# Loading the second stage's first tiles into the first stage's input and output buffers

## The chip, the cores and the metric

The kernel runs on one core of a Trainium2 chip. The time is the device time of one execution in microseconds (us); a timing is the median over its runs. The profile is that of one more execution, whose own time is given beside its span.

## The reference

The input x is 32 images of 256 channels and 56 x 56 pixels (M = 3136), float32. Two layers are computed. Cut to what matters:

```python
# layer 0, over all images at once: im is (256, 32*3136)
im = relu(x); mn = mean(im); im = im - mn
p = clip(u.T @ im, -clampVal, clampVal)
scale = 255 / (max(p) - min(p))            # one per row, over all images
p = round((p - min(p)) * scale) / scale + min(p)
p = u @ p;  y = p - mean(p) + mn
# layer 1, per image
h = relu(bn(w_conv1 @ y)); d = relu(bn(w_dr @ h + b_dr))
cov = covariance of d over the pixels;  att = sigmoid(w_fc @ rowconv(bn(cov)) + b_fc)
out = y * att
```

The minimum and the maximum of p over all 32 images have to be known before anything can be quantised, and so the work falls into stages.

## The kernel before

The two sets of 128 channels (K = 2) lie on the 128 partitions. The kernel has three blocks, and each ends with a barrier that all five engines meet.

**First stage** (a span of 565 us): p = u.T @ relu(x) for all images. An image goes through in four pieces (SUBS = 4) of 784 pixels (S). SP, the engine that only issues transfers here, loads each piece into `xs[:, k]` once GpSimd has read the piece that was there (`split_done`). ScalarE applies the relu in place and makes the coarse part `xh`, GpSimd makes the rest `xl`, TensorE multiplies, and VectorE moves the result out of PSUM while it takes maximum and minimum. For the first NL = 28 images the result goes into one of four buffers `po[k]` and from there SP stores it to DRAM (`p0_dram`); `p_stored[k]` counts the stores that have landed. Two of these buffers are `po_low`, two lie in the long-lived buffer `late`. The last RES = 4 images stay in SBUF (`p_res`) and are not stored. They are taken one after every seven stored images, so that the last image of the stage is one that stays: behind the last store there is a whole image of work with no transfer in it.

**Second stage** (566 to 803 us): every p is quantised to a byte so that the bytes can be summed, and the weights of the third stage are prepared. First VectorE reduces the statistics, and TensorE multiplies the mean by u (`shift_ps`); from these come `lo` and `qa`, the offset and the scale of the quantisation, which every tile needs. Then the 56 stored tiles (28 images x 2 channel sets, each 128 x 3136 numbers, 1568 KB) are brought back through four places (TILES = 4) `pt[:, t]`: SP issues four loads at the stage's start (L393), and then one more whenever VectorE has quantised the tile in that place (`quantised`, L398). VectorE quantises a tile into `qt` (L530), and ScalarE reads the bytes and sums them (L470). The four kept images are quantised and summed in the same way without a load (L537, L464).

The order on each engine is written out by hand. Between the groups of four tiles (`two_samples`) stand the steps of the weight preparation, and they pass back and forth between the engines: ScalarE copies `w1u_ps` (L481) behind the first four sums; VectorE scales the weights with it (L549, L550); ScalarE takes absolute values (L485, L486) behind the next five sums; TensorE sums them (L435); VectorE makes scales of them (L556 to L577); ScalarE takes `absv` (L490) behind five more sums; TensorE L446, VectorE L592 to L600, TensorE L450, VectorE L603 to L611. Only then does VectorE enter the loops in which nothing but tiles is worked on.

**Third stage** (803 us to the end): for each image the outputs and the attention are computed from the bytes, which are made anew from a reload of p. TensorE bounds it.

Of the kernel before, what the change touches and what calls it, by code (L numbers as in the profile page):

```python
# [29 lines left out]
P = 128  # L30
# [9 lines left out]
def wait_from(eng, semaphore, value):  # L40

    if not (isinstance(value, int) and value <= 0):
        eng.wait_ge(semaphore, value)


def layer_kernel(nc, x, u, clamp, w1, g1, b1, wdr, b_dr, g_dr, be_dr, g_row, be_row,
                 w_row, b_row, w_fc, b_fc, out):
    N, C, HH, WW = x.shape
    M = HH * WW
    K = C // P  # L50
    J = w_row.shape[1]
    RES = 4
    NL = N - RES
# [4 lines left out]
    p0_dram = nc.dram_tensor("p0_scratch", [N, K, P, M], F32, kind="Internal").ap()  # L58
    p0_v = p0_dram.rearrange("n k p m -> n p k m")

    with ExitStack() as ctx:
        def sb(name, shape, dt=F32, stack=ctx):
            return stack.enter_context(nc.sbuf_tensor(name, shape, dt))
# [4 lines left out]
        def sem(name):  # L68
            return ctx.enter_context(nc.semaphore(name))
# [51 lines left out]
        lo = sb("lo", [P, K])  # L121
# [8 lines left out]
        SUBS = 4  # L130
        S = M // SUBS
# [12 lines left out]
        stats = ExitStack()  # L144
        xsum = sb("xsum", [P, K, N * SUBS], stack=stats)
        pmax = sb("pmax", [P, K, N * SUBS], stack=stats)
        pmin = sb("pmin", [P, K, N * SUBS], stack=stats)

        x_loaded = [sem(f"x_loaded{k}") for k in range(SUBS)]
        p_stored = [sem(f"p_stored{k}") for k in range(SUBS)]  # L150
        u_split, relu_done, high_done, split_done = (sem("u_split"), sem("relu_done"), sem("high_done"),
                                                     sem("split_done"))
# [1 line left out]
        scaled = sem("scaled")  # L154

        with ExitStack() as a:
            xs = sb("xs", [P, SUBS, K, S], stack=a)
            xh = sb("xh", [P, 2, K, S], F32R, stack=a)
            xl = sb("xl", [P, 2, K, S], F32R, stack=a)
            po_low = sb("po_low", [P, 2, K, S], stack=a)  # L160
            po_late = late[:, 0:2 * K * S].rearrange("p (b k s) -> p b k s", b=2, k=K)
            po = [po_low[:, 0], po_low[:, 1], po_late[:, 0], po_late[:, 1]]
            uh = sb("uh", [P, K, C], F32R, stack=a)
# [8 lines left out]
            @block.sync  # L172
            def _(sp):
                sp.dma_start(u_sb[:], u.rearrange("(k p) j -> p k j", p=P)).then_inc(u_loaded, 16)
                for k in range(SUBS):
                    sp.dma_start(xs[:, k], x_v[0, :, :, k * S:(k + 1) * S]).then_inc(x_loaded[k], 16)
                for dst, src in [
                    (w1_sb[:], w1.rearrange("(k p) o -> p k o", p=P)), (wdr_sb[:], wdr),
                    (wrow_sb[:], w_row), (wfc_sb[:], w_fc.rearrange("(k p) n -> p k n", p=P)),
                    (brow_sb[:], b_row.rearrange("(p j) -> p j", j=J)),  # L180
                ]:
                    sp.dma_start(dst, src).then_inc(params_loaded, 16)
                for dst, src in [(cv, clamp), (g1_sb, g1), (b1_sb, b1), (bfc_sb, b_fc)]:
                    for k in range(K):
                        sp.dma_start(dst[:, k:k + 1], src[k * P:(k + 1) * P].rearrange("(p o) -> p o", o=1)
                                     ).then_inc(params_loaded, 16)
                for dst, src in [(bdr_sb, b_dr), (gdr_sb, g_dr), (bedr_sb, be_dr), (grow_sb, g_row),
                                 (berow_sb, be_row)]:
                    sp.dma_start(dst[:], src.rearrange("(p o) -> p o", o=1)).then_inc(params_loaded, 16)

                def load(n, turn, k):

                    sp.wait_ge(split_done, SUBS * (turn - 1) + k + 1)
                    sp.dma_start(xs[:, k], x_v[n, :, :, k * S:(k + 1) * S]).then_inc(x_loaded[k], 16)

                def store(n, k):
                    sp.wait_ge(p_ready, SUBS * n + k + 1)
                    sp.dma_start(p0_v[n, :, :, k * S:(k + 1) * S], po[k]).then_inc(p_stored[k], 16)


                def load_and_store(n_load, n_store, turn, first=False):
                    for k in range(SUBS):
                        load(n_load, turn, k)
                        if k > 0:
                            store(n_store, k - 1)
                        elif not first:
                            store(n_store - 1, SUBS - 1)

                def group(r, more):
                    load_and_store(PER * r + 1, PER * r, (PER + 1) * r + 1, first=True)  # L210
                    with sp.Fori(1, PER - 1) as s:
                        load_and_store(PER * r + s + 1, PER * r + s, (PER + 1) * r + s + 1)
                    load_and_store(NL + r, PER * r + PER - 1, (PER + 1) * r + PER)
                    if more:
                        load(PER * r + PER, (PER + 1) * r + PER + 1, 0)
                    store(PER * r + PER - 1, SUBS - 1)
                    if more:
                        for k in range(1, SUBS):
                            load(PER * r + PER, (PER + 1) * r + PER + 1, k)

                with sp.Fori(0, RES - 1) as r:
                    group(r, True)
                group(RES - 1, False)

            @block.scalar
            def _(act):
# [123 lines left out]
                    resident_sample(r, (PER + 1) * r + PER)  # L350


        TILES = 2 * K
        PAIRS = NL // 2

        p_loaded = [sem(f"p_loaded{t}") for t in range(TILES)]
        mean_done, shift_done = sem("mean_done"), sem("shift_done")
        res_quantised, res_summed = sem("res_quantised"), sem("res_summed")
        quantised, summed = sem("quantised"), sem("summed")
# [3 lines left out]
        rows_made, rows_spread = sem("rows_made"), sem("rows_spread")  # L363

        with ExitStack() as b:
            pt = sb("pt", [P, TILES, M], stack=b)
            qt = sb("qt", [P, TILES, M], U8, stack=b)
            hi = sb("hi", [P, K], stack=b)
            same = sb("same", [P, K], stack=b)
# [17 lines left out]

            @block.sync
            def _(sp):
                for k in range(SUBS):  # L390
                    sp.wait_ge(p_stored[k], 16 * NL + 16)
                for t in range(TILES):
                    sp.dma_start(pt[:, t], p0_dram[t // K, t % K]).then_inc(p_loaded[t], 16)  # L393

                with sp.Fori(0, NL - 2, 2) as n:
                    for t in range(TILES):
                        sp.wait_ge(quantised, K * n + t + 1)
                        sp.dma_start(pt[:, t], p0_dram[n + 2 + t // K, t % K]).then_inc(p_loaded[t], 16)  # L398

            @block.tensor  # L400
            def _(pe):
# [52 lines left out]
            def _(act):  # L454
# [12 lines left out]
                def two_samples(p):  # L467
                    for t in range(TILES):
                        act.wait_ge(quantised, TILES * p + t + 1)
                        nc.scalar.activation(qt[:, t], qt[:, t], ACT.Copy,  # L470
                                             accum_out=qsum[:, t % K, bass.ds(2 * p + t // K, 1)]
                                             ).then_inc(summed, 1)

                def round_of_pairs(i):
                    for h in range(2):
                        resident_tile(i, h)
                        two_samples(2 * i + h + 1)
# [13 lines left out]
                with act.Fori(1, RES) as i:  # L491
                    round_of_pairs(i)
                with act.Fori(2 * RES + 1, PAIRS) as p:
                    two_samples(p)

            @block.vector
            def _(dve):
# [28 lines left out]
                def two_samples(i):  # L526
                    for t in range(TILES):
                        dve.wait_ge(p_loaded[t], 16 * (i + 1))
                        wait_from(dve, summed, TILES * (i - 1) + t + 1)
                        nc.vector.tensor_scalar(qt[:, t], pt[:, t], lo[:, t % K:t % K + 1],  # L530
                                                qa[:, t % K:t % K + 1], ALU.subtract, ALU.mult).then_inc(quantised, 1)

                def resident_tile(i, h):
# [6 lines left out]
                def round_of_pairs(i):  # L540
                    for h in range(2):
                        resident_tile(i, h)
                        two_samples(2 * i + h + 1)

                two_samples(0)

                dve.wait_ge(turned_read, 2)
# [3 lines left out]
                last.then_inc(scaled_w, 1)  # L551
                resident_tile(0, 0)
                two_samples(1)

                dve.wait_ge(sums_done, 1)
# [59 lines left out]
                with dve.Fori(1, RES) as i:  # L615
                    round_of_pairs(i)
                with dve.Fori(2 * RES + 1, PAIRS) as p:
                    two_samples(p)
# [26 lines left out]
        with ExitStack() as c_:  # L645
# [285 lines left out]
            def _(dve):  # L931
                steps = [0]

                def settle(ins):
                    steps[0] += 1
                    ins.then_inc(prepare_step, 1)
                    dve.wait_ge(prepare_step, steps[0])
# [18 lines left out]
                nc.vector.memset(gg[:], 1.0)  # L956
                dve.wait_ge(summed, TILES * PAIRS)
                settle(nc.vector.tensor_reduce(mq, qsum[:], AX_X, ALU.add))
# [117 lines left out]
```

## Time and profile before

| | |
|---|---|
| median of 3 runs | 1931.46 us (1931.35 to 1931.91) |
| the profiled execution's own time | 1932.07 us |
| its span, first to last instruction | 1930.3 us |
| TensorE busy | 1677.6 us (87%) |
| VectorE busy | 1530.7 us (79%) |
| ScalarE busy | 1498.2 us (78%) |
| GpSimd busy | 460.4 us (24%), all in the first stage: 459.6 us of it in its 128 pieces |
| mean granted TensorE clock | 0.935 of full speed |
| first, second, third stage | to 565.6, 565.6 to 802.8, from 802.8 us |

In the profile PE is TensorE, PEld its weight loads, DVE is VectorE, ACT is ScalarE, POOL is GpSimd, SP issues the transfers; a q behind an engine's name is its sequencer. Times are counted from the span's start. A line L530 is line 530 of the kernel before. What an idle engine waited for is written with an arrow, as [1.44 <-DMA ...].

### The profile page before, as it was taken

What the parts mean: (1) busy time and instruction counts of PE and PEld (TensorE: products, weight loads), DVE (VectorE), ACT (ScalarE), POOL (GpSimd) and SP (SyncE); (2) the same over time, 40 slices, a digit from 0 to 9 for tenths busy, and PEclk for the clock granted to TensorE, in tenths of its full rate; (3) what the DMA queues carried; (4) which work ended last, traced back from release to release, by engine and by line L of the source; (5) the groups of instructions that cost most, each with busy time, mean ns of one, the idle gap of its engine ahead of it and who ended that gap; (6) DMA issues with size and microseconds to landing.
All of it is one profiled execution on the core that took longest, in us unless ns stands there. A gap on an engine that the chain in (4) does not pass through costs nothing.

```text
span 1930.3 us, 40083 instructions
## 1 busy us (share of the span) xinstructions
PE 1677.6 (87%) x13394; PEld 1319.8 (68%) x13394; DVE 1530.7 (79%) x2801; ACT 1498.2 (78%) x2270; POOL 460.4 (24%) x135
## 2 busy tenths in 40 slices
PE   8999999999981000289999999999999999999998
PEld 8999999999981000156666666666676666666664
DVE  5888888888875664466888888888888888888883
ACT  6777777777756897568788887878878888787886
POOL 6888888888840000000000000000000000000000
PEclk9999999999985555599999999999999999999999
DMA  9998999989968899601364554645546455554634
GB/s 326 377 365 315 372 339 343 374 316 366 374 260 346 351 425 426 280 2 68 128 230 164 194 195 154 236 154 210 181 164 224 160 213 175 177 207 160 228 113 201
DMA packets 139341, 477.35 MB, mean 247 GB/s; under 512 B 10528, under 2 KB 33184, under 8 KB 124192
## 3 DMA queue, kind: packets, MB, share of 16 engines
q1 hardware_dynamic: 139296, 476.75, 67.2%
q8 instruction: 28, 0.46, 0.1%
q14 instruction: 17, 0.14, 0.0%
HBM read 284.04 MB, written 192.68 MB: 247 GB/s over the span
## 4 chain that ended last, share of the span: by engine, by line
PE 55%; ACT 1%; DVE 1%; issue 1%; ACTq 0%
PE y_ps L829 18%; PE z_ps L855 17%; PE d_ps L805 13%; PE cov_ps L786 5%; PE ch_ps L840 1%; ACT h L896 1%; ACT hh L901 0%; PE ch_ps L818 0%; PE ch_ps L817 0%; DVE g L1046 0%; PE cov_ps L789 0%; ACT p_res L924 0%; DVE hl L1037 0%; PE ch_ps L764 0%; PE cov_ps L770 0%
## 5 line engine op out<-in xcount | busy, mean ns | idle before, releaser
L278 POOL TENSOR_TENSOR xl<-xs,xh 128x1568 fp32r<-128x1568 f32 x128 | 459.6, 3591 | 97.8 <-ACT xh L238 97.8
L1037 DVE TENSOR_TENSOR hl<-h,hh 128x1024 f16<-128x1024 f32 (+2 forms) x224 | 244.1, 1090 | 102.9 <-ACT hh L901 102.7
L829 PE MATMUL y_ps<-qr,udh 128*128 128x512 f16 (+2 forms) x896 | 313.5, 353 | 4.0 <-ACT p_res L924 3.6
L855 PE MATMUL z_ps<-qr,wl 128*128 128x512 f16 (+2 forms) x896 | 314.1, 354 | 0.0
L855 PE MATMUL z_ps<-qr,wh 128*128 128x512 f16 (+2 forms) x896 | 314.0, 353 | 0.0
L829 PE MATMUL y_ps<-qr,udl 128*128 128x512 f16 (+2 forms) x896 | 313.0, 352 | 0.0
L924 ACT ACTIVATE p_res<-y_ps,att_cy 128x512 f32<-128x512 f32 (+2 forms) x448 | 298.2, 713 | 9.5 <-PE y_ps L829 4.5
L238 ACT ACTIVATE xh<-xs 128x1568 fp32r<-128x1568 f32 x128 | 194.1, 1517 | 140.6 <-PE pp L295 140.6
L896 ACT ACTIVATE h<-z_ps,sb_h 128x512 f32<-128x512 f32 (+2 forms) x448 | 264.4, 627 | 30.6 <-PE z_ps L855 26.8
L805 PE MATMUL d_ps<-vh,hh 128*128 128x128 f16 (+1 forms) x1600 | 282.3, 220 | 2.5 <-DVE hl L1037 2.3
L805 PE MATMUL d_ps<-vh,hl 128*128 128x128 f16 (+1 forms) x1600 | 281.6, 219 | 0.0
L805 PE MATMUL d_ps<-vl,hh 128*128 128x128 f16 (+1 forms) x1600 | 281.5, 219 | 0.0
L295 PE MATMUL pp<-xh,uh 128*128 128x392 f32 x1024 | 267.6, 342 | 9.2 <-ACT xh L238 9.2
L295 PE MATMUL pp<-xh,ul 128*128 128x392 f32 x1024 | 266.9, 342 | 0.0
L888 ACT ACTIVATE gg<-g 128x512 f16<-128x512 f32 (+1 forms) x224 | 130.8, 584 | 175.2 <-DVE g L1046 175.2
L329 DVE TENSOR_REDUCE pmin<-pp 128x784 f32 x256 | 248.3, 970 | 0.0
L901 ACT ACTIVATE hh<-h 128x1024 f16<-128x1024 f32 (+2 forms) x224 | 212.8, 950 | 7.1
L232 ACT ACTIVATE xs<-xs 128x784 f32<-128x784 f32 x256 | 215.3, 843 | 3.7 <-DMA xs<-in_x_dram 3.7
L295 PE MATMUL pp<-xl,uh 128*128 128x392 f32 x1024 | 204.8, 342 | 0.0
L295 PEld LDWEIGHTS pp<-xh,uh 128*128 128x128 f32 x1024 | 188.8, 189 | 9.2 <-issue 9.2
L295 PEld LDWEIGHTS pp<-xh,ul 128*128 128x128 f32 x1024 | 189.2, 189 | 0.0
L295 PEld LDWEIGHTS pp<-xl,uh 128*128 128x128 f32 x1024 | 185.5, 188 | 0.0
(164 smaller groups left out, 2820.7 us busy)
## 6 DMA issues: line engine op xcount, KB each, us to landing
xs<-in_x_dram SPq DMA_DIRECT2D x128, 784.0 KB, 6.8
out_dram<-p_res SPq DMA_DIRECT2D x31, 3136.0 KB, 10.3
pt<-p_scratch SPq DMA_DIRECT2D x56, 1568.0 KB, 12.9
p_res<-p_scratch SPq DMA_DIRECT2D x112, 512.0 KB, 4.6
p_scratch<-po_low SPq DMA_DIRECT2D x56, 784.0 KB, 7.7
p_scratch<-late SPq DMA_DIRECT2D x56, 784.0 KB, 7.7
p_res<-p_scratch SPq DMA_DIRECT2D x56, 384.0 KB, 3.2
p_res<-p_scratch SPq DMA_DIRECT2D x28, 320.0 KB, 3.3
```

The costliest lines, as they stand in the source:

```text
L232: last = nc.scalar.activation(xs[:, k, m], xs[:, k, m], ACT.Relu, accum_out=xsum[:, m, bass.ds(g, 1)])
L238: nc.scalar.activation(xh[:, k % 2], xs[:, k], ACT.Copy).then_inc(high_done, 1)
L278: nc.gpsimd.tensor_tensor(xl[:, k % 2], xs[:, k], xh[:, k % 2].bitcast(F32), ALU.subtract).then_inc(split_done, 1)
L295: last = nc.tensor.matmul(pp[:, k % 2, m, c, 0:SC], lhs, rhs[:, c * SC:(c + 1) * SC], start=first and n == 0, stop=final and n == len(part ...
L329: nc.vector.tensor_reduce(pmin[:, m, bass.ds(g, 1)], p_psum(k, m), AX_XY, ALU.min).then_inc(psum_read, 1)
L805: last = nc.tensor.matmul(d_ps[0:q, par, t], lhs, rhs, start=n == 0, stop=n == len(parts) - 1)
L829: last = nc.tensor.matmul(y_ps[:, m, 0:widths[c]], part[:, k, m * P:(m + 1) * P], qr[:, slot, k, columns(c)], start=k == 0 and part is udh ...
L855: last = nc.tensor.matmul(z_ps[:, m, 0:w], part[:, k, m * P:(m + 1) * P], qr[:, a, k, columns(s)], start=k == 0 and part is wh, stop=k == ...
L896: nc.scalar.activation(h32[:, par, m, 0:w], z_ps[:, m, 0:w], ACT.Relu, bias=sb_h[:, m:m + 1]).then_inc(z_read, 1)
L901: nc.scalar.activation(hh[:, par, :, 0:w], h32[:, par, :, 0:w], ACT.Copy).then_inc(hh_done, 1)
L924: nc.scalar.activation(yo[:, slot, m, columns(c)], y_ps[:, m, 0:widths[c]], ACT.Identity, scale=att_cy[:, m, 0:1], bias=att_cy[:, m, 1:2]) ...
L1037: nc.vector.tensor_tensor(hl[:, par, :, 0:w], h32[:, par, :, 0:w], hh[:, par, :, 0:w], ALU.subtract).then_inc(h_split, 1)
```

## The change

The tile places of the second stage are laid over buffers of the first. A new buffer `early`, 128 x 3 x 3136, lives through both. In the first stage `early[:, 0]` is the pair `po_low`, and `early[:, 1:3]` are the four x pieces: pieces 0 and 1 fill the second of the three parts, pieces 2 and 3 the third. In the second stage the three parts are the places of tiles 0, 1 and 2; the fourth is the new `late_tile`, which only the second stage has. The total is what it was, since `xs`, `po_low` and `pt` are no longer buffers of their own.

The first three loads move from the start of the second block to the end of the first block's SP program. Tile 0 waits for all stores of the first stage to have landed, tile 1 for GpSimd to have read pieces 0 and 1 of the last image, tile 2 for it to have read all four. The fourth load stays where it was.

```diff
+        EARLY = TILES - 1
+        early = sb("early", [P, EARLY, M], stack=stats)
...
-            xs = sb("xs", [P, SUBS, K, S], stack=a)
+            xs = early[:, 1:3].rearrange("p t m -> p (t m)").rearrange("p (u k s) -> p u k s", u=SUBS, k=K)
...
-            po_low = sb("po_low", [P, 2, K, S], stack=a)
+            po_low = early[:, 0].rearrange("p (b k s) -> p b k s", b=2, k=K)
...
+                def load_p(t):
+                    sp.dma_start(early[:, t], p0_dram[t // K, t % K]).then_inc(p_loaded[t], 16)
+
+                for k in range(SUBS):
+                    sp.wait_ge(p_stored[k], 16 * NL + 16)
+                load_p(0)
+                sp.wait_ge(split_done, SUBS * (N - 1) + 2)
+                load_p(1)
+                sp.wait_ge(split_done, SUBS * N)
+                load_p(2)
...
-            pt = sb("pt", [P, TILES, M], stack=b)
+            late_tile = sb("late_tile", [P, M], stack=b)
+            pt = [early[:, t] for t in range(EARLY)] + [late_tile[:]]
...
-                for k in range(SUBS):
-                    sp.wait_ge(p_stored[k], 16 * NL + 16)
-                for t in range(TILES):
-                    sp.dma_start(pt[:, t], p0_dram[t // K, t % K]).then_inc(p_loaded[t], 16)
+                sp.dma_start(pt[EARLY], p0_dram[EARLY // K, EARLY % K]).then_inc(p_loaded[EARLY], 16)
```

Here is SP's program around the barrier between the first and the second stage, before the change. L194 loads an x piece, L198 stores a p piece, L156 is the branch out of the first block, and L393 and L398 are the loads of tiles.

```order
L194 DMA xs<-in_x_dram 128x2x784 [waits split_done]
L198 DMA p_scratch<-late 128x2x784 [waits p_ready] x2
L156 UNCONDITIONAL_BRANCH
L388 UNCONDITIONAL_BRANCH [waits barrier_Pool_Activation_PE_DVE_SP_release]
L393 DMA pt<-p_scratch 128x3136 [waits p_stored2,p_stored3,p_stored1,p_stored0]
L393 DMA pt<-p_scratch 128x3136 x3
L395 UNCONDITIONAL_BRANCH
L395 ISA
L398 ISA [waits quantised]
L398 DMA pt<-p_scratch 128x3136
```

And the same place after it, where L201, L205, L163 and L411 are the former L194, L198, L156 and L398, and L234 and L406 the former L393.

```order
L201 DMA early<-in_x_dram 128x2x784 [waits split_done]
L205 DMA p_scratch<-late 128x2x784 [waits p_ready] x2
L234 DMA early<-p_scratch 128x3136 [waits p_stored2,p_stored3,p_stored1,p_stored0]
L234 DMA early<-p_scratch 128x3136 [waits split_done] x2
L163 UNCONDITIONAL_BRANCH
L404 UNCONDITIONAL_BRANCH [waits barrier_Pool_Activation_PE_DVE_SP_release]
L406 DMA late_tile<-p_scratch 128x3136
L408 UNCONDITIONAL_BRANCH
L408 ISA
L411 ISA [waits quantised]
L411 DMA early<-p_scratch 128x3136
```

Three loads with their waits now stand ahead of the barrier; one stays behind it, and the loop of reloads is as before.

VectorE's program at the start of the second stage, after the last step that makes `lo` and `qa`, before the change:

```order
L524 TENSOR_SCALAR qa<-hi 128x2
L530 TENSOR_SCALAR qt<-pt,lo,qa 128x3136 [waits p_loaded0,vec_step]
L530 TENSOR_SCALAR qt<-pt,lo,qa 128x3136 [waits p_loaded1]
L530 TENSOR_SCALAR qt<-pt,lo,qa 128x3136 [waits p_loaded2]
L530 TENSOR_SCALAR qt<-pt,lo,qa 128x3136 [waits p_loaded3]
L549 TENSOR_SCALAR late<-late,inv 128x256 [waits turned_read]
```

And after it:

```order
L537 TENSOR_SCALAR qa<-hi 128x2
L543 TENSOR_SCALAR qt<-early,lo,qa 128x3136 [waits p_loaded0,vec_step]
L543 TENSOR_SCALAR qt<-early,lo,qa 128x3136 [waits p_loaded1]
L543 TENSOR_SCALAR qt<-early,lo,qa 128x3136 [waits p_loaded2]
L543 TENSOR_SCALAR qt<-late_tile,lo,qa 128x3136 [waits p_loaded3]
L562 TENSOR_SCALAR late<-late,inv 128x256 [waits turned_read]
```

The order and the waits are the same; only the places of the tiles have other names. The programs of ScalarE, TensorE and GpSimd differ in names alone as well.

## Rows read from the trace of the kernel before

**Rows 1.** Busy time by stretch; behind the engines granted TensorE clock, DMA share, GB/s:

```profile
551.50:565.60 14.10, 10.67 (x60) 10.36 (x59) 11.83 (x21) 6.83 (x25) 6.73 (x2) 0.97 0.00 2
...
615.00:620.00 5.00, 2.08 (x2) 0.50 (x2) 4.96 (x11) 1.87 (x1) 0.00 (x0) 0.50 0.01 2
...
640.00:645.00 5.00, 0.00 (x0) 0.00 (x0) 5.00 (x3) 3.04 (x3) 0.00 (x0) 0.50 0.17 30
...
650.80:797.60 146.80, 0.00 (x0) 0.00 (x0) 81.90 (x45) 129.51 (x91) 0.00 (x0) 0.50 1.00 422
```

**Rows 2.** VectorE in order of time (start, duration, what, idle before and its releaser):

```profile
571.57 0.16 DVE L524 TENSOR_SCALAR qa<-hi 128x2 f32<-128x2 f32 x1
573.16 1.91 DVE L530 TENSOR_SCALAR qt<-pt,lo,qa 128x3136 uint8<-128x3136 f32 x1 [1.44 <-DMA pt<-p_scratch]
...
584.42 1.91 DVE L530 TENSOR_SCALAR qt<-pt,lo,qa 128x3136 uint8<-128x3136 f32 x1 [1.87 <-DMA pt<-p_scratch]
589.80 0.35 DVE L549 TENSOR_SCALAR late<-late,inv 128x256 f32<-128x256 f32 x1 [3.46 <-ACT late L481]
```

**Rows 3.** ScalarE in order of time over the same stretch:

```profile
571.32 1.02 ACT L460 ACTIVATE late<-wfc_ps 128x1024 f32<-128x1024 f32 x1 [1.95 <-PE wfc_ps L421]
575.11 2.82 ACT L470 ACTIVATE qt<-qt 128x3136 uint8<-128x3136 uint8 x1 [2.76 <-DVE qt L530]
...
586.37 2.82 ACT L470 ACTIVATE qt<-qt 128x3136 uint8<-128x3136 uint8 x1 [0.87 <-DVE qt L530]
...
589.19 0.58 ACT L481 ACTIVATE late<-w1u_ps 128x512 f32<-128x512 f32 x1
...
595.61 2.80 ACT L470 ACTIVATE qt<-qt 128x3136 uint8<-128x3136 uint8 x1
...
606.81 0.61 ACT L485 ACTIVATE u_sb<-late 128x512 f32<-128x512 f32 x1
```

**Rows 4.** The later steps of the weight preparation, from the same view of three engines:

```profile
571.08 3.62 PE L427 MATMUL w1u_ps<-late,u_sb 128*128 128x256 f32 x8
...
607.99 1.01 PE L435 MATMUL shift_ps<-ones,w_sb 128*128 128x1 f32 x4 [33.29 <-ACT w_sb L486]
...
613.30 0.16 DVE L556 TENSOR_TENSOR small<-b_sb,shift_ps 128x2 f32<-128x2 f32 x1 [11.87 <-PE shift_ps L435]
...
618.13 2.82 ACT L464 ACTIVATE q_first<-q_first 128x3136 uint8<-128x3136 uint8 x1 [10.19 <-DVE q_first L537]
...
633.64 0.16 DVE L592 SCALAR_TENSOR_TENSOR small<-shift_ps,small 128x1 f32<-128x1 f32 x1 [4.81 <-PE shift_ps L446]
...
641.72 7.37 DVE L530 TENSOR_SCALAR qt<-pt,lo,qa 128x3136 uint8<-128x3136 f32 x4
```

**Rows 5.** VectorE where the tiles alone are left, and its last tile:

```profile
654.18 1.91 DVE L530 TENSOR_SCALAR qt<-pt,lo,qa 128x3136 uint8<-128x3136 f32 x1 [1.45 <-DMA pt<-p_scratch]
...
797.58 1.91 DVE L530 TENSOR_SCALAR qt<-pt,lo,qa 128x3136 uint8<-128x3136 f32 x1 [1.85 <-DMA pt<-p_scratch]
```

**Rows 6.** SP's issues, its wait at the barrier, GpSimd's last piece:

```profile
542.91 4.69 SPq L198 DMA_DIRECT2D p_scratch<-late  x2
565.69 2.24 SPq L393 DMA_DIRECT2D pt<-p_scratch  x4
...
SPq L156 <- PEq L156: 17.7, 1, 17.7
...
555.37 3.58 POOL L278 TENSOR_TENSOR xl<-xs,xh 128x1568 fp32r<-128x1568 f32 x1 [0.72 <-ACT xh L238]
```

**Rows 7.** Issue to landing (the tile loads; 540 to 575 us), instruction transfers (570 to 576 us):

```profile
DMA to landing us min/median/max: 6.3/12.9/17.4
...
pt<-p_scratch SPq DMA_DIRECT2D x4, 1568.0 KB, 12.4
p_scratch<-late SPq DMA_DIRECT2D x2, 784.0 KB, 6.5
...
q8 instruction: 1, 0.02, 0.9%
```

More of the change, by code:

```diff
@@ L147, in layer_kernel @@
         pmin = sb("pmin", [P, K, N * SUBS], stack=stats)
+        TILES = 2 * K
+        PAIRS = NL // 2
+        EARLY = TILES - 1
+        early = sb("early", [P, EARLY, M], stack=stats)
+        assert SUBS == TILES and SUBS * S == M
         x_loaded = [sem(f"x_loaded{k}") for k in range(SUBS)]
+        p_loaded = [sem(f"p_loaded{t}") for t in range(TILES)]
         p_stored = [sem(f"p_stored{k}") for k in range(SUBS)]
@@ L350, in _ @@
                     resident_sample(r, (PER + 1) * r + PER)
-        TILES = 2 * K
-        PAIRS = NL // 2
-        p_loaded = [sem(f"p_loaded{t}") for t in range(TILES)]
         mean_done, shift_done = sem("mean_done"), sem("shift_done")
@@ L397, in _ @@
                         sp.wait_ge(quantised, K * n + t + 1)
-                        sp.dma_start(pt[:, t], p0_dram[n + 2 + t // K, t % K]).then_inc(p_loaded[t], 16)
+                        sp.dma_start(pt[t], p0_dram[n + 2 + t // K, t % K]).then_inc(p_loaded[t], 16)
             @block.tensor
@@ L529, in two_samples @@
                         wait_from(dve, summed, TILES * (i - 1) + t + 1)
-                        nc.vector.tensor_scalar(qt[:, t], pt[:, t], lo[:, t % K:t % K + 1],
+                        nc.vector.tensor_scalar(qt[:, t], pt[t], lo[:, t % K:t % K + 1],
                                                 qa[:, t % K:t % K + 1], ALU.subtract, ALU.mult).then_inc(quantised, 1)
```

## Prediction

> **What bounds the kernel now.** I read the table of the engines first: TensorE is busy for 87% of the span, but the change touches none of its work. The stretches come next, since a busy share is a mean over stages. In the second stage TensorE is nearly idle, and its time is set in one part by the transfers and in another by the weight preparation. From 650.80 to 797.60 us the DMA share is 1.00 at 422 GB/s; from 615 to 620 it is 0.01 and from 640 to 645 it is 0.17 [rows 1]. The reader is to see in this that the stage has two regimes. Up to 641.7 us the transfers run ahead of the engines, fill the four places and stop. After that they are the limit: VectorE's tile at 654.18 and the last at 797.58 wait for a load, with 38 steps between them, so (797.58 - 654.18) / 38 = 3.77 us a tile [rows 5].
>
> Second, the order of time on VectorE and ScalarE at the stage's start. VectorE makes `qa` at 571.57 and then waits 1.44 us for the first load; it starts the fourth tile at 584.42, after 1.87 us of waiting for its load; that is 11.26 us for three steps, the 3.77 of the loads again. Then it waits 3.46 us for ScalarE's copy L481, until 589.80 [rows 2]. ScalarE sums the first tile at 575.11 and the fourth at 586.37, idle before that one for 0.87 us, and makes the copy at 589.19 [rows 3]. This chain was late because of loads. Behind it there is not one load on the path up to 641.72: ScalarE's sums follow each other without a gap from 595.61 to the absolute values at 606.81 [rows 3]; TensorE (607.99), VectorE (613.30), ScalarE (618.13), VectorE (633.64) wait for one another, and VectorE's four tiles from 641.72 take 7.37 us with no wait inside them [rows 4].
>
> Third, SP: it issued the last two stores from 542.91 on and stood at the barrier for 17.7 us [rows 6], while the DMA share was 0.00 for 14.1 us [rows 1].
>
> **The change part by part.** All times below are in the profiled execution.
>
> Issue of the early loads. The last store was issued at about 542.91 + 4.69 - 0.39 = 547.2, and the last two took 6.5 us in the median to land [rows 6, 7]: 553.7. Then tile 0 is issued; tile 1 with it, since GpSimd read piece 1 of the last image two pieces before the one it starts at 555.37; tile 2 at 555.37 + 3.58 = 558.95 [rows 6]. SP needs under a microsecond for each issue (2.24 us for four [rows 6]) and is at the barrier by about 560, 5 us before it opens. Nothing is queued behind these waits on SP, since its last store is out, and no other transfer is wanted until 565.6.
>
> Landing. Over the 56 tile loads the time to landing was 6.3 us at least and 17.4 at most, queueing behind others included; the four at the stage's start had a median of 12.4 [rows 7]. The first of those four was issued at 565.69 and used at 573.16 [rows 2, 6], 7.5 us. So tile 0 lands near 561, tile 1 near 565, tile 2 near 569 (3.77 after the one before it or 7.5 after its issue, whichever is later, with some for queueing), and `late_tile`, alone in the queue from 565.7, near 573.2.
>
> VectorE. L521 to L524 come with steps of 0.2 us behind one another where one waits for the one before, so tile 0 starts at 571.57 + 0.20 = 571.77 in place of 573.16. Four tiles back to back take 7.37 us [rows 4], a step of (7.37 - 1.91) / 3 = 1.82: they start at 571.8, 573.6, 575.4 and 577.2. Every load above is there by then, the tightest by 4 us.
>
> ScalarE is now the slower of the two. It is free at 571.32 + 1.02 = 572.34 and starts 0.04 us behind a tile's end (573.16 + 1.91 against 575.11): at 573.72. Its own step is (606.81 - 595.61) / 4 = 2.80 [rows 3], so the fourth sum starts at 582.12 and copy L481 at 584.94. What the copy reads was made by TensorE by 571.08 + 3.62 = 574.70 [rows 4]. VectorE goes on 0.61 us after the copy's start, at 585.55 in place of 589.80. The saving: 1.39 us from the earlier first tile, 2.86 us because four sums start within 8.40 us in place of 11.26; **4.25 us**. The whole 15 us that the first four loads took is not to be had: 11.3 of it, three tiles by 3.77, is taken off SP's queue, and ScalarE's sums, hidden beside the loads before, become the limit after 4.25 of it.
>
> From there to 641.72. Each link moves by the same 4.25 us if no load is late. The loads of the second four follow the quantising of the first four, from 573.7 on: with 7.5 us for the first and 3.77 for each further one they land at 581.2, 585.0, 588.7 and 592.5, and VectorE wants them at 588.4, 590.3, 592.1 and 593.9 (592.67, 594.49 and so on before, each less 4.25; 592.67 is 589.80 with its four scalings and one kept tile). ScalarE, which is the path here, wants the last of them quantised only by 599.8. For the third and the fourth group both the places and their users move together, and the queue ran dry before both already [rows 1]. TensorE's few products at 607.99 come after 33.29 us of idleness [rows 4]; now it is 29, and the granted clock there is 0.50 in every one of these stretches [rows 1], so they cost the same.
>
> From 641.72 on. The four places are full in both kernels when VectorE gets there, so the head start of the loads is used up: a fifth tile can't be loaded ahead. The 40 tiles left go at 3.77 each from a start that is 4.25 us earlier. The last tile, the barrier and the third stage move with it.
>
> The other edits (a view in place of a buffer, other addresses, the same four places) change no instruction in number or shape; I cost them at 0. The traffic of the early loads lies beside the last image's work. GpSimd's step there is 3.58 us at a DMA share of 0.00 [rows 6, 1], and 459.6 / 128 = 3.59 in the mean over all its pieces, nearly all with the queues full, so I take nothing for it.
>
> Bounds. Above: if `lo` and `qa` were not the limit either, ScalarE's sums could start at 572.34, 1.4 us earlier, but they need them; so 4.3 is the upper end of this mechanism. Below: a late `late_tile` costs nothing until it is quantised after 582.12, so until it lands after 580.2, which is 14.5 us behind its issue; at the longest landing time of the trace, 17.4, it would cost 2.9 us, and the gain would be 1.4. I take the row of a load issued into an empty queue, 7.5 us, as the nearest. To both sides I add 0.6 us, the spread of the three runs.
>
> The sum: 1932.07 - 4.25 = 1927.8 us for an execution like the profiled one. That one is 0.61 us over the median of the runs, so the median is forecast at 1931.46 - 4.25 = 1927.2 us, 0.22% faster. A change of 0.2%, 3.9 us, is about what a measurement of this kernel can tell from none.
>
> **The rivals.** *The transfers set the whole stage.* The share of 1.00 over 147 us speaks for it. Then all three tiles count: 3 x 3.77 = 11.3 us, 1920.2 us. Against it are the two dry stretches of the queue [rows 1] and the 10.19 us and 11.87 us that ScalarE and VectorE wait for one another in between [rows 4]. Chance 0.04.
>
> *A smaller gain.* Some link between 589.80 and 641.72 doesn't follow, or a load lands late: 1.4 to 3.5 us are left, 1928 to 1930. No row shows a link that hangs on something else, but the view names only the last releaser of each wait. Chance 0.12.
>
> *The barrier waits for the loads.* If the end of a block holds until the transfers of SP's queue have landed, the second stage starts when tile 2 is in. Landed at 569 that is 3.4 us later than 565.6, and the gain is 0.9 us, 1930.6; at 12.4 us behind its issue at 559 it is 571.4, a loss of 1.5, 1933.0; the gain is gone from a landing at 569.9 on. The rows say little against it, as the stores before had landed 12 us before the barrier. In its favour I see only that no row excludes it. Chance 0.05.
>
> *Slower: code waits behind the loads.* All engines branch into the second block at 565.6, until now with empty queues. If one of them must fetch code there, and the fetch stands in line behind two tile loads, the stage's first steps, which lead to `qa`, come 2 x 3.77 = 7.5 us later; less 4.25 that is a loss of 3.3 us, 1934.8. It decides from a delay of 4.25 us on. Against it: an instruction transfer lies in the stretch from 570 to 576, with the queues full [rows 7], and no engine stood still for it there. The Trainium skill ("DMA: Bandwidth & Descriptors", section "Queues, rings and completion order") says that each DMA engine takes turns between the queue rows that have work, a packet at a time; by that rule the fetch would not stand behind whole tiles, and the time would be that of the forecast. The trace agrees as far as it goes, by that one transfer. Chance 0.04.
>
> **How the numbers follow.** The forecast, 1927.2 us, has 0.75 with its own range 1926.6 to 1928.2. The range for 8 in 10 reaches up into the smaller gain and leaves out the rest: 1926.2 to 1929.6. Faster by over 0.2% means under 1927.6: some 0.87 of the forecast's chance, since it lies only 0.4 us beyond, and the case of 11 us: 0.69. Within 0.2%: the rest of the forecast, the smaller gain and nearly all of the barrier's and the code's cases: 0.27. Slower by over 0.2% needs a delay of over 8 us: 0.04.
>
> **What would show it.** In the profile of the changed kernel: VectorE's first tile near 571.8 with no wait for a load, the next three 1.8 us apart; ScalarE's four sums without a gap; L562 (the former L549) near 585.6; the group of four at 641.72 now near 637.5; the last tile near 793.3; the barrier still at 565.6. I am wrong if the barrier opens later, if VectorE still waits for a load among the first four, if the DMA share does not fall to nothing once more around 611 to 616, or if the 4.25 us at 585.6 are not the same 4.25 us at 637.5.

## The result and the profile after

The changed kernel takes 1926.10 us in the median of 8 runs (1924.81 to 1927.39); the kernel before, run beside it, 1931.40 us (1929.61 to 1932.67, 8 runs). The ratio is 0.9972, 95% interval 0.9961 to 0.9983: 5.4 us faster, between 3.3 and 7.5. Forecast were 1927.2 us and a gain of 4.25 us; the gain lies in the interval, the time 0.1 us under the lower end of my range, 1926.2. With eight runs the median is the middle of the fourth and the fifth, 1925.34 and 1926.86, and no run took a time between these two. The profiled execution took 1926.86 us, its span is 1925.1 us.

The stretches of the changed kernel, in the columns of [rows 1] (the last three are granted clock, DMA share and GB/s):

```profile
551.50:565.60 14.10, 10.66 (x60) 10.36 (x59) 11.81 (x20) 6.69 (x24) 6.58 (x2) 0.95 0.84 338
...
610.00:615.00 5.00, 2.07 (x2) 0.50 (x2) 4.90 (x13) 1.28 (x1) 0.00 (x0) 0.50 0.00 2
635.00:640.00 5.00, 0.00 (x0) 0.00 (x0) 5.00 (x6) 2.43 (x1) 0.00 (x0) 0.50 0.00 0
...
646.50:793.30 146.80, 0.00 (x0) 0.00 (x0) 82.14 (x45) 129.66 (x91) 0.00 (x0) 0.50 1.00 421
```

Against [rows 1] the reader sees the DMA engines busy ahead of the barrier, which they were not, and the same two dry stretches, some 5 us earlier. VectorE, to be set beside [rows 2]:

```profile
571.42 0.16 DVE L537 TENSOR_SCALAR qa<-hi 128x2 f32<-128x2 f32 x1
571.62 5.56 DVE L543 TENSOR_SCALAR qt<-early,lo,qa 128x3136 uint8<-128x3136 f32 x3
577.09 1.91 DVE L543 TENSOR_SCALAR qt<-late_tile,lo,qa 128x3136 uint8<-128x3136 f32 x1
585.38 0.35 DVE L562 TENSOR_SCALAR late<-late,inv 128x256 f32<-128x256 f32 x1 [6.38 <-ACT late L494]
```

The waits for the four loads are gone, and the wait for ScalarE's copy has grown from 3.46 to 6.38 us: the gain of VectorE was 7.3 us at the fourth tile and is 4.4 us behind the copy. ScalarE, beside [rows 3]:

```profile
573.56 2.82 ACT L483 ACTIVATE qt<-qt 128x3136 uint8<-128x3136 uint8 x1 [1.37 <-DVE qt L543]
...
581.98 2.80 ACT L483 ACTIVATE qt<-qt 128x3136 uint8<-128x3136 uint8 x1
...
584.77 0.57 ACT L494 ACTIVATE late<-w1u_ps 128x512 f32<-128x512 f32 x1
```

Its first and fourth sum start 8.42 us apart, against 11.26 before. The later links, beside [rows 4, 5]:

```profile
603.58 1.02 PE L448 MATMUL shift_ps<-ones,w_sb 128*128 128x1 f32 x4 [29.03 <-ACT w_sb L499]
...
608.89 0.16 DVE L569 TENSOR_TENSOR small<-b_sb,shift_ps 128x2 f32<-128x2 f32 x1 [13.26 <-PE shift_ps L448]
...
629.24 0.16 DVE L605 SCALAR_TENSOR_TENSOR small<-shift_ps,small 128x1 f32<-128x1 f32 x1 [4.81 <-PE shift_ps L459]
...
637.33 5.55 DVE L543 TENSOR_SCALAR qt<-early,lo,qa 128x3136 uint8<-128x3136 f32 x3
...
792.99 1.91 DVE L543 TENSOR_SCALAR qt<-late_tile,lo,qa 128x3136 uint8<-128x3136 f32 x1 [1.84 <-DMA late_tile<-p_scratch]
```

The first stage ends at a slightly different time in each execution, so I count from the barrier, that is from VectorE's first reduction behind it:

```profile
565.62 0.42 DVE L506 TENSOR_REDUCE mn<-xsum 128x2 f32<-128x256 f32 x1 [0.33 <-PEq L156]
```

```profile
565.47 0.42 DVE L519 TENSOR_REDUCE mn<-xsum 128x2 f32<-128x256 f32 x1 [0.33 <-PEq L163]
```

The first is before, the second after. The table has these distances for every kernel of the study (us; "weights" is the first scaling behind ScalarE's copy, "last tile" VectorE's last in the second stage).

| kernel | VectorE's first reduction at | first tile | weights | last tile | median us |
|---|---|---|---|---|---|
| before | 565.62 | +7.54 | +24.18 | +231.96 | 1931.40 |
| after | 565.47 | +6.15 | +19.91 | +227.52 | 1926.10 |
| e1, after again | 565.35 | +6.14 | +19.91 | +227.81 | 1925.73 |
| e2, overlay alone | 564.25 | +7.44 | +24.05 | +231.72 | 1931.38 |
| e3, one tile early | 564.91 | +4.49 | +20.21 | +227.95 | 1927.29 (one run) |
| e4, copy earlier | 565.97 | +6.15 | +14.32 | +224.66 | 1924.50 |
| w1, after and matmuls | 565.15 | +4.35 | +18.12 | +225.81 | 1924.50 |
| w2, before and matmuls | 564.58 | +7.28 | +23.89 | +231.52 | 1930.13 |
| a1, after, steps ahead | 564.90 | +4.43 | +12.60 | +208.36 | 1908.66 |
| a2, before, steps ahead | 566.80 | +7.32 | +20.41 | +217.88 | 1917.02 |
| b1, after, both | 564.66 | +4.35 | +12.52 | +208.65 | 1907.65 |

In the two profiled executions the spans differ by 5.2 us. Of that 4.3 us are there at the weights and 4.4 at the last tile. The rest is not shown to be the change's: the barrier is 0.15 us earlier, the third stage gives 0.3 us back (ScalarE's last output starts at 1924.96 before and at 1920.66 after, 4.30 apart), and the last store took 3.9 us to land before and 3.0 after, 0.9 us:

```profile
out_dram<-p_res SPq DMA_DIRECT2D x1, 320.0 KB, 3.9
```

```profile
out_dram<-p_res SPq DMA_DIRECT2D x1, 320.0 KB, 3.0
```

### The profile page after: what moved, and what is told of

Same layout as the page of the kernel before. It is cut to its first block, busy times and chain, and to the rows that moved or that the text cites. A ratio compares the mean times of both kernels' runs of the same rounds, so it can differ in the third digit from the quotient of the medians.

```text
span 1925.1 us, 40083 instructions
## 1 busy us (share of the span) xinstructions
PE 1677.5 (87%) x13394; PEld 1319.3 (69%) x13394; DVE 1530.7 (80%) x2801; ACT 1497.2 (78%) x2270; POOL 459.9 (24%) x135
## 4 chain that ended last, share of the span: by engine, by line
PE 55%; ACT 1%; DVE 1%; issue 1%; ACTq 0%
PE y_ps L842 18%; PE z_ps L868 17%; PE d_ps L818 13%; PE cov_ps L799 5%; ACT h L909 1%; PE ch_ps L853 1%; ACT hh L914 0%; PE ch_ps L831 0%; DVE g L1059 0%; PE ch_ps L830 0%; PE cov_ps L802 0%; ACT p_res L937 0%; DVE hl L1050 0%; ACT gg L901 0%; PE ch_ps L777 0%
## 5 line engine op out<-in xcount | busy, mean ns | idle before, releaser
L297 POOL TENSOR_TENSOR xl<-early,xh 128x1568 fp32r<-128x1568 f32 x128 | 459.1, 3587 | 98.1 <-ACT xh L257 98.1
L257 ACT ACTIVATE xh<-early 128x1568 fp32r<-128x1568 f32 x128 | 194.1, 1516 | 140.2 <-PE pp L314 140.1
L251 ACT ACTIVATE early<-early 128x784 f32<-128x784 f32 x256 | 215.2, 842 | 3.9 <-DMA early<-in_x_dram 3.9
```

The source lines that it names most:

```text
L251: last = nc.scalar.activation(xs[:, k, m], xs[:, k, m], ACT.Relu, accum_out=xsum[:, m, bass.ds(g, 1)])
L257: nc.scalar.activation(xh[:, k % 2], xs[:, k], ACT.Copy).then_inc(high_done, 1)
L297: nc.gpsimd.tensor_tensor(xl[:, k % 2], xs[:, k], xh[:, k % 2].bitcast(F32), ALU.subtract).then_inc(split_done, 1)
```

## The experiments

**e1, the changed kernel again, and e2, the overlay without the early loads** (ratio to before 0.9972, 0.9960 to 0.9983, and 1.0000, 0.9991 to 1.0009). The edit of e2:

```diff
-                load_p(0)
-                sp.wait_ge(split_done, SUBS * (N - 1) + 2)
-                load_p(1)
-                sp.wait_ge(split_done, SUBS * N)
-                load_p(2)
...
-                sp.dma_start(pt[EARLY], p0_dram[EARLY // K, EARLY % K]).then_inc(p_loaded[EARLY], 16)
+                for t in range(TILES):
+                    sp.dma_start(pt[t], p0_dram[t // K, t % K]).then_inc(p_loaded[t], 16)
```

> The changed kernel once more, unaltered. Theory (the early loads bring 4.25 us, fixed by ScalarE's four sums; all beyond it is variation between executions): VectorE goes on behind the copy L494 19.9 us after the barrier, as in the profile of after (585.38 - 565.47), and the loops start 4.25 us earlier than before by the same measure; the five timed pairs differ by 3 to 6 us and the runs of one kernel spread by 2 to 3 us. Rival (a lasting further gain of 1 us from the new layout or from less traffic): the median of the pairs is again 5.2 us or more.

> The change without its early loads: the four tile places lie over the first stage's buffers, but all four loads are issued behind the barrier, as before. Theory: nothing but the early issue matters, so VectorE's first tile starts 7.6 us behind the barrier again, the copy ends the wait 24.2 us behind it, and the time is that of before, within the runs' spread (0 us, -1 to +1). Rival (the layout brings the extra 1 us): 1 us less than before.

The layout brings nothing: e2 is at the time of before, and its first tile waits for its load again. In e1 the profile repeats the 4.27 us at the weights, but the median is 5.3 us under before again, as the rival of e1 had it. Neither interval excludes 4.25 us, so the extra microsecond is not shown by the medians; that it came twice was reason to look closer. The single times say where. The changed kernel's 15 runs (8 and 7) fall into two groups: 8 from 1924.81 to 1925.73, 7 from 1926.86 to 1927.65, and none between. Both profiled executions are of the upper group. Its middle is 1927.4, beside my 1927.2; that of the lower group is 1925.3.

**e3, one tile early.** Only `load_p(0)` stays ahead of the barrier; the other three loads are issued behind it. There is one timed run, so only its profile is used.

> Tile 0 alone is loaded early; tiles 1 to 3 are issued behind the barrier. Theory (ScalarE's sums at 2.80 us a tile take over as the limit): the loads of tiles 1 to 3 land 7.5, 11.3 and 15.0 us behind the barrier, VectorE has them quantised in time for ScalarE's second and third sum, and only the fourth is late, by 0.6 us. VectorE goes on behind the copy 20.5 us after the barrier: 3.6 of the 4.25 us are there with one tile of three. Rival (every early tile brings its equal share): 22.8 us after the barrier, a gain of 1.4 us.

The weights come at +20.21: one tile of three brings 3.97 of the 4.27 us, so equal shares are wrong. It does not show ScalarE's pace, since here the loads still set it. VectorE's third and fourth tile wait for theirs, and ScalarE waits 0.87 us before its fourth sum:

```profile
579.74 1.91 DVE L540 TENSOR_SCALAR qt<-late_tile,lo,qa 128x3136 uint8<-128x3136 f32 x1 [1.87 <-DMA late_tile<-p_scratch]
581.69 2.82 ACT L480 ACTIVATE qt<-qt 128x3136 uint8<-128x3136 uint8 x1 [0.87 <-DVE qt L540]
```

And the first tile starts at +4.49, not at +6.15. That was not expected, and it is the clue:

```profile
564.90 0.30 PE L415 MATMUL w_ps<-ident,w_sb 128*128 128x128 f32 x1 [3.44 <-PEq L163]
...
566.02 1.08 PE L426 MATMUL shift_ps<-mn,u_sb 128*128 128x1 f32 x8
...
567.22 0.16 DVE L522 TENSOR_TENSOR hi<-hi,shift_ps 128x2 f32<-128x2 f32 x1 [1.04 <-PE shift_ps L426]
```

In the profile of after the same three steps read:

```profile
565.46 0.44 PE L418 MATMUL w_ps<-ident,w_sb 128*128 128x128 f32 x1 [3.44 <-PEq L163]
...
567.62 1.70 PE L429 MATMUL shift_ps<-mn,u_sb 128*128 128x1 f32 x8
...
569.44 0.16 DVE L525 TENSOR_TENSOR hi<-hi,shift_ps 128x2 f32<-128x2 f32 x1 [2.70 <-PE shift_ps L429]
```

TensorE had idled for the same 3.44 us in both, but in e3 the clock had not fallen yet when the second stage began. The granted clock from 564 to 566 us and from 566 to 568 us (after first, then e3):

```profile
564.00:566.00 2.00, 0.54 (x3) 0.57 (x4) 1.63 (x5) 0.00 (x0) 0.00 (x0) 0.55 0.88 376
566.00:568.00 2.00, 2.00 (x12) 2.00 (x10) 0.74 (x3) 0.14 (x1) 0.00 (x0) 0.50 0.85 194
```

```profile
564.00:566.00 2.00, 1.10 (x10) 1.13 (x11) 1.63 (x5) 0.00 (x0) 0.00 (x0) 1.00 0.28 50
566.00:568.00 2.00, 2.00 (x15) 2.00 (x14) 0.86 (x6) 1.36 (x3) 0.00 (x0) 0.67 0.82 270
```

The share of 0.50 is 1.2 GHz, that of 1.00 is 2.4 GHz. In e3, where the clock fell between 566 and 568 us, in the middle of these steps, the first tile comes 1.66 us sooner than in after; in w1 below, at 2.4 GHz throughout, 1.80 us. Before, this was hidden: the first tile waited for its load until +7.5. After, these steps are on the path.

**e4, ScalarE's copy earlier.**

```diff
-                two_samples(0)
+                two_samples(0, 0, 2)
                 act.wait_ge(turned, 3)
                 nc.scalar.activation(w1u_t[:], w1u_ps[:], ACT.Copy).then_inc(turned_read, 1)
+                two_samples(0, 2)
```

> The changed kernel, with ScalarE's copy of w1u (L494) moved from behind its four first sums to behind the second. Theory (the four sums ahead of the copy are what is left on the path): VectorE gets its weights at about 14.3 us behind the barrier in place of 19.9, the kept tile no longer makes ScalarE wait 3.03 us, the absolute values come 3.1 us earlier, and the loops start 3.1 us earlier: a time 7 to 8 us under before. Rival (the loads of the second group are the limit as soon as ScalarE is not): the second group waits for its loads and under 1 us comes of it.

Ratio 0.9959 (0.9946 to 0.9972), 7.9 us by the ratio and 6.6 by the medians (1931.06 - 1924.50); 7 to 8 were expected, and the intervals of e4 and after overlap, so the difference between the two kernels rests on the profiles. The weights come at +14.32, where 14.3 was expected, and the last tile 2.9 us earlier than in after. ScalarE's sums ahead of the copy were what limited the gain:

```profile
580.29 0.35 DVE L563 TENSOR_SCALAR late<-late,inv 128x256 f32<-128x256 f32 x1 [0.79 <-ACT late L494]
```

The rival's wait for the second group's loads is there too, 1.30 and 1.87 us on its third and fourth tile, but ScalarE is not held up by it.

**w1 and w2, a busy TensorE up to the barrier**, in the kernel after and in the kernel before. The edit adds work whose result is not used:

```diff
+                pe.wait_ge(psum_read, K * (SUBS * N - 1))
+                for n in range(17):
+                    nc.tensor.matmul(pp[:, 0, 0, 0, 0:SC], uh[:, 0, 0:P], xh[:, 0, 0, 0:SC],
+                                     start=True, stop=True)
```

> The changed kernel with 17 matmuls more at the end of TensorE's first block; they fill the 3.4 us in which it has nothing to do before the barrier, and their result is used by nobody. Theory (the second stage's first steps are now on the path, and they run at whichever clock is granted at the barrier, which is why the runs of after fall into two groups 2 us apart): TensorE's steps up to the product for the shift run at full clock in every execution, VectorE's first tile starts 4.5 us behind the barrier and not 6.15, and the median is that of the lower group of after, 1924.5 to 1925.3. Rival (the two groups come from elsewhere, the third stage for one): two groups again, median 1925.7 to 1926.1.

> The kernel before with the same 17 matmuls. Theory: its first tile waits for its load, which lands 7.5 us behind the barrier whatever the clock, so the quicker first steps bring nothing; first tile 7.4 to 7.6 us behind the barrier, time within 0.5 us of before. Rival (the clock helps either kernel): 1.6 us under before.

w1: ratio 0.9965 (0.9951 to 0.9979), median 1924.50 us, and one group from 1923.97 to 1925.22. The ratio alone does not tell w1 from after, whose interval overlaps; the single group of five and the profile do the telling. The idle time before the barrier's release is 0.42 us and the first steps run at full clock:

```profile
561.54 3.18 PE L336 MATMUL pp<-xh,uh 128*128 128x392 f32 x17
565.14 0.30 PE L423 MATMUL w_ps<-ident,w_sb 128*128 128x128 f32 x1 [0.42 <-PEq L163]
...
566.26 0.95 PE L434 MATMUL shift_ps<-mn,u_sb 128*128 128x1 f32 x8
```

With the first tile 1.80 us sooner than in after the weights come 1.79 us sooner, at +18.12: ScalarE's four sums set that distance. Of the 2.9 us between the two profiled executions 1.7 are there at the last tile; 0.3 lie in the first stage and 0.9 in the third.

w2: ratio 0.9994 (0.9985 to 1.0003). Its steps are as quick, but VectorE waits longer for the load, 2.97 us in place of 1.44:

```profile
566.75 0.16 DVE L517 TENSOR_TENSOR hi<-hi,shift_ps 128x2 f32<-128x2 f32 x1 [0.91 <-PE shift_ps L421]
571.86 1.91 DVE L535 TENSOR_SCALAR qt<-pt,lo,qa 128x3136 uint8<-128x3136 f32 x1 [2.97 <-DMA pt<-p_scratch]
```

The distance to the first tile is 0.12 us under the range expected. The median, 1.3 us under that of before, misses the expected 0.5 and does not settle it by itself: the interval holds 0 and also the rival's 1.6 us. The profile speaks for the theory: w2's last tile is only 0.44 us closer to the barrier than that of before, where w1's is 1.71 closer than that of after.

**a1 and a2, ScalarE's steps ahead of the sums**, again in both kernels. Besides the edit of e4:

```diff
-                resident_tile(0, 0)
-                two_samples(1)
                 act.wait_ge(scaled_w, 1)
                 nc.scalar.activation(absu[:], ud32[:], ACT.Abs)
                 nc.scalar.activation(absw[:], w32[:], ACT.Abs).then_inc(abs_done, 1)
-                resident_tile(0, 1)
-                two_samples(2)
+                resident_tile(0, 0)
+                two_samples(1)
                 act.wait_ge(scaled_v, 1)
                 nc.scalar.activation(absv, v32[:], ACT.Abs).then_inc(abs_done, 1)
+                resident_tile(0, 1)
+                two_samples(2)
```

> The changed kernel with ScalarE's steps of the weight preparation each moved ahead of a group of sums: the copy of w1u behind the second sum, the absolute values of u and w1 ahead of the second group, that of v ahead of the third. Theory (what kept the queue of loads dry around 612 and 638 us were these steps waiting behind the sums): the loads run on with hardly a gap from 573.7 us, the last tile is quantised 209 to 215 us behind the barrier in place of 227.5, the time is 1908 to 1915 us. Rival (with ScalarE's sums at 2.80 us a tile and five tiles a group, ScalarE itself sets the pace): 220 us or more behind the barrier, 1919 us or more.

> The same moves of ScalarE's steps in the kernel before. Theory: now the loads set nearly the whole stage, so the early loads are worth more than the 4.25 us they bring after: the kernel before with the moves has its last tile 216 to 222 us behind the barrier, 7 us later than the changed kernel with them, and takes 1915 to 1922 us. Rival (the early loads bring 4.25 us in any setting): the two differ by 4.25 us. A second one (they bring all three tiles, 11.3 us): they differ by 11.3 us.

a1: ratio 0.9884 (0.9868 to 0.9899), 1908.66 us; a2: 0.9926 (0.9912 to 0.9939), 1917.02 us. The queue of loads is full, or nearly so, where it was dry; in a1:

```profile
605.00:610.00 5.00, 0.00 (x0) 0.00 (x0) 4.86 (x12) 5.00 (x5) 0.00 (x0) 0.50 1.00 418
610.00:615.00 5.00, 1.65 (x2) 0.50 (x2) 3.19 (x15) 2.41 (x2) 0.00 (x0) 0.50 1.01 427
615.00:620.00 5.00, 0.00 (x0) 0.00 (x0) 5.00 (x7) 2.15 (x1) 0.00 (x0) 0.50 0.65 273
```

Early loads are now worth 8.4 us by the medians (1917.02 - 1908.66) and 9.5 at the last tile, neither 4.25 nor 11.3. I had expected 7. The profile of a1 has its first tile at +4.43, which is 1.7 us less than the +6.15 that I had reckoned with, and 7 + 1.7 = 8.7 is in line with it. a1's four times are again two pairs: 1907.21 and 1907.65, the first of them the profiled execution with the full clock, and 1909.66 and 1909.89. The lower pair is 9.6 us under a2's median, the upper 7.2. That the last tile comes 0.6 us earlier than the 209 to 215 probably has the same cause.

**b1, both.**

> Both together on the changed kernel: ScalarE's steps ahead of the groups of sums, and the 17 matmuls before the barrier. Theory: every execution has its first tile 4.35 us behind the barrier, as the profile of w1 had, and the last 208 us behind it; one group of times in place of a1's two (1907.2 and 1907.7, 1909.7 and 1909.9), median 1906.8 to 1907.8. Rival (the matmuls help only while ScalarE's sums are on the path, and the loads are the limit now): median as a1's, 1908.7, and two groups.

1907.65 us, ratio 0.9876 (0.9860 to 0.9893), the fastest kernel here. Its 4 runs lie within 0.6 us (1907.42 to 1908.01), a1's 4 within 2.7. That supports the clock as the cause of the two groups, though four runs each are few, and the medians differ by only 1.0 us.

## Why the prediction's mechanism held, and what failed in it

The early issue: right. SP issued tiles 0 and 1 at 552.9 (I had 553.7) and tile 2 at 558.8, was at the barrier at about 559.4 and waited there 6.0 us:

```profile
552.88 6.28 SPq L234 DMA_DIRECT2D early<-p_scratch  x3
565.42 0.33 SPq L406 DMA_DIRECT2D late_tile<-p_scratch  x1
...
SPq L163 <- PEq L163: 6.0, 1, 6.0
```

The landings: 6.8 and 10.2 us behind the issue for the first two, 8.4 for tile 2 and 7.3 for `late_tile`. So tile 2 landed at 567.2 and `late_tile` at 572.7, ahead of their use at 575.3 and 577.1.

The barrier waiting for the loads: wrong. Tile 2 landed at 558.8 + 8.4 = 567.2, and the barrier opened at 565.47, with 0.33 us between VectorE's last step and its first as before. Code waiting behind the loads: wrong, since `qa` is made 5.95 us behind VectorE's first reduction in both kernels (571.57 - 565.62 and 571.42 - 565.47). The transfers setting the whole stage: wrong in this kernel, the queue ran dry twice; with ScalarE's steps moved (a1 and a2) the early loads bring 9.5 us at the last tile, 1.7 of it by the clock, where this rival had 11.3.

ScalarE's takeover, 4.25 us at the weights, the same at 637.3 and at the last tile: right. By the barrier's clock 4.27, 4.24 (76.10 against 71.86) and 4.44 us were measured. That ScalarE's sums are the reason is shown by e4, in which two sums fewer stand ahead of the copy, and by w1, in which the weights move with the first tile. Expected marks were 571.8, 585.6, 637.5 and 793.3 us, measured 571.6, 585.4, 637.3 and 793.0, with the barrier itself 0.15 us earlier.

What failed is the upper bound of the gain, and with it the lower end of the range: "if `lo` and `qa` were not the limit either, ScalarE's sums could start at 572.34, 1.4 us earlier, but they need them; so 4.3 is the upper end of this mechanism." I took the 6.15 us from the barrier to the first tile from one execution as if they were fixed. They are 6.14 or 6.15 in the three profiles (after, e1, e4) in which the clock had fallen to 1.2 GHz at the barrier. Where it fell later they are 4.43 and 4.49 (a1, e3), and 4.35 where it did not fall in these steps (w1, b1): the gain is up to 1.8 us larger. The copy of `wfc_ps` at 571.32, which I named as ScalarE's earliest start, moves with TensorE's clock too: it is at 5.70 us behind VectorE's first reduction before and at 4.04 in e3. It was in my rows: the stretch from 551.50 has a granted clock of 0.97, the later ones 0.50, so the fall lay near the barrier. What was hidden under a wait for a load could differ from run to run without being seen. The other term that was too small is the 0.6 us for the spread, taken from three runs of before: over 8 runs before alone spread by 3.1 us. None of the four signs by which I had said I would be wrong appeared, and none of them looked at the clock.

So the median is no single number but depends on how many runs fall into which group: 1927.4 us in the group that I forecast, 1925.3 in the other, with 7 and 8 of 15 runs. By how much it missed my range is luck, to either side. With one more of the eight runs in the upper group the median would have been 1926.86 or more, inside the range; with one more in the lower it would have been under 1925.8, as in e1.

How far are the two groups shown to be two moments of the clock's fall? w1's five runs form one group, at or under the lower one; b1's four form one, beside a1's lower pair; and the profiled execution of a1, with the full clock at the barrier, is in that lower pair. The mean granted clock of each run points the same way without separating them: 0.936 or 0.937 in the 8 runs of the lower group, 0.935 in three and 0.936 in four of the upper. But no profiled execution of the unaltered kernel fell into the lower group, so for it the link stays indirect. Nor is the whole distance explained: the first steps give 1.7 to 1.8 us of the 2.1 between the middles of the groups. The kernel before spreads by 3.1 us although its first tile waits for a load, and a2, built on it, has a gap of 1.5 us between its third and fourth time. So part of the spread comes from elsewhere. The traces show two places. One is the first stage, told of in the last section. The other is the third: from VectorE's first step in it to the end of the span it takes 1126.0 us in the profile of w1 and 1127.5 in that of e1.

## What to carry to other kernels

When loads are brought forward, the gain ends where the next engine in line takes over; find its step time and count from when it is free. A stream that is limiting later on gets faster only by as much as its last dry stretch moves, so look first at why it runs dry: here moving three small ScalarE steps ahead of the long sums brought 17 us on top, against 5 us for the loads. And when a wait is removed, whatever was hidden beneath it comes onto the path with all its variation; read its granted clock before calling it constant. Look at the single times too, and not only at their median: a gap among them can mean that two kinds of execution are mixed.

## What the runs showed of the hardware

With the same program on TensorE and the same 3.44 us in which it was idle, the granted clock from 564 to 566 us was 1.00 in one execution (e3) and 0.55 in another (after). The Trainium skill ("TensorE: Matmul & The Clock Gate", section "Part 1: The HAM clock gate") says that what sets the clock does not start anew with the kernel, so that the moment of the change varies between runs. The traces agree, in the fall at the barrier and also in the rise at the start. Two matmuls of the first stage take 0.85 us at 1.2 GHz and 0.52 us at 2.4 GHz. In e2 (the first two lines) the change is between 11.3 and 12.5 us, in before (the other two) between 13.9 and 16.3:

```profile
11.27 0.85 PE L309 MATMUL pp<-xh,ul 128*128 128x392 f32 x2
12.46 0.51 PE L309 MATMUL pp<-xh,ul 128*128 128x392 f32 x2
...
13.94 0.85 PE L295 MATMUL pp<-xh,ul 128*128 128x392 f32 x2
...
16.32 0.52 PE L295 MATMUL pp<-xh,uh 128*128 128x392 f32 x2
```

In e2 the barrier opens 1.4 us earlier than in before (564.25 against 565.62), and the clock falls behind it and not ahead of it. It is so in all eight profiles without the added matmuls: in the three in which the clock fell behind the barrier (e2, e3, a1) VectorE's first reduction is at 564.25 to 564.91, in the five in which it had fallen before (before, after, e1, e4, a2) at 565.35 to 566.80. So an execution that is quick behind the barrier tends to be quick ahead of it as well.

Seventeen matmuls of 0.19 us each, put where nobody waits for them, kept the granted clock at full speed through the barrier in all three profiles in which they were tried (w1, w2, b1).

A load of 1568 KB issued into an empty queue landed 6.8 us later (the single early load of e3). The later ones of after, with others in flight ahead of them, took 7.3 to 10.2 us. In a full stream there is one every 3.77 us.
